# Perceiver block on one Trainium2 core: ten units of the V projection placed earlier in the instruction streams

## The reference, cut to what matters

```
x = x + depool(layernorm(x), ctx, lens)
x = x + mamba(layernorm(x))            # delta = softplus(...), scan over 64 tokens, 16 states
x = x + bitnet_ffn(layernorm(x))       # ternary weights, activations quantized per row
x = x + cross_attention(layernorm(x), ctx)   # K, V = ctx @ Wkv (16 heads of 64)
x = x + head_attention(layernorm(x))
x = x + experts(layernorm(x))
```

## Time and profile before

| | |
|---|---|
| median of 3 runs | 3235.72 us (3234.48 to 3242.55) |
| the profiled execution's own time | 3228.4 us |
| its span, first to last instruction | 3226.7 us |
| mean granted clock of TensorE | 0.957 of full |
| TensorE busy | 2927.9 us, 91% |
| VectorE busy | 1506.7 us, 47% |
| ScalarE busy | 1012.3 us, 31% |
| `mamba_in` softplus to its end | about 151 to 229 us |
| `mamba_scan` | 229 to 696.6 us |
| `mamba_out` and norm n2 | 696.6 to 753.6 us |
| `bitnet` | 753.6 to 910.6 us |
| `queries` with n3 | 910.6 to about 1415 us |

### The profile page before, as it was taken

The page is one execution under the profiler, slowest core; times in us unless marked ns, Lnnn a source line. Parts: engine busy times, 40 slices in busy tenths (PEclk is TensorE's granted clock), DMA queues, the critical chain, the costliest instruction groups (busy, mean ns, idle before and its releaser), DMA issues. The chain is left out here.

```text
span 3226.7 us, 40186 instructions
## 1 busy us (share of the span) xinstructions
PE 2927.9 (91%) x17021; PEld 1616.3 (50%) x17029; DVE 1506.7 (47%) x1769; ACT 1012.3 (31%) x1525; POOL 68.6 (2%) x189
## 2 busy tenths in 40 slices
PE   6979999977989999989999999999999997636799
PEld 3324444433444444446666666666666664415453
DVE  5359999974633222333434343434343432376410
ACT  3344334313422221222323232323232321284210
POOL 1000000000000000000000000000000000010000
PEclk9989999988999999999999999999999998867999
DMA  5123343333323333444556554546464543102203
GB/s 198 59 73 92 93 145 89 92 101 140 96 91 121 102 99 103 129 116 110 142 115 143 114 143 110 143 114 143 112 143 110 117 84 85 53 20 46 95 10 143
DMA packets 472619, 341.52 MB, mean 106 GB/s; under 512 B 232212, under 2 KB 437333, under 8 KB 467832
## 3 DMA queue, kind: packets, MB, share of 16 engines
q1 hardware_dynamic: 472440, 338.95, 38.7%
HBM read 226.60 MB, written 54.62 MB: 87 GB/s over the span
## 5 line engine op out<-in xcount | busy, mean ns | idle before, releaser
L366 PE MATMUL vw_pv<-vw_wv,vw_ctx 128*128 128x512 f16 (+1 forms) x1296 | 496.8, 383 | 63.0 <-DVE vw_vst L386 27.6
L367 PE MATMUL vw_pv<-vw_wv,vw_ctx 128*128 128x512 f16 (+1 forms) x1296 | 496.4, 383 | 0.0
L368 PE MATMUL vw_pv<-vw_wv,vw_ctx 128*128 128x512 f16 (+1 forms) x1296 | 495.5, 382 | 0.0
L1442 PE MATMUL ca_p_s<-early_halves,ca_qw 128*128 128x448 f16 (+2 forms) x1408 | 466.7, 331 | 1.4 <-DVE ca_qw L1555 1.4
L1443 PE MATMUL ca_p_s<-early_halves,ca_qw 128*128 128x448 f16 (+2 forms) x1408 | 466.7, 331 | 0.0
L1444 PE MATMUL ca_p_s<-early_halves,ca_qw 128*128 128x448 f16 (+2 forms) x1408 | 466.6, 331 | 0.0
L1555 DVE TENSOR_TENSOR ca_qw<-ca_p_w,ca_qw 128x512 f16<-128x512 f32 x128 | 88.5, 691 | 545.6 <-ACT ca_qw L1505 545.6
L386 DVE TENSOR_TENSOR vw_vst<-vw_pv,vw_vst 128x512 f16<-128x512 f32 x162 | 110.8, 688 | 376.9 <-ACT vw_vst L377 376.8
L1505 ACT ACTIVATE ca_qw<-ca_p_w 128x512 f16<-128x512 f32 x128 | 76.4, 597 | 558.8 <-PE ca_p_w L1423 558.8
L377 ACT ACTIVATE vw_vst<-vw_pv 128x512 f16<-128x512 f32 x162 | 95.4, 593 | 468.4 <-PE vw_pv L368 468.4
L366 PEld LDWEIGHTS vw_pv<-vw_wv,vw_ctx 128*128 128x128 f16 (+1 forms) x1296 | 127.7, 99 | 228.9 <-issue 39.9
(11 more groups left out here) (439 smaller groups left out, 4700.3 us busy)
## 6 DMA issues: line engine op xcount, KB each, us to landing
vw_ring<-in_ctx_t SPq DMA_DIRECT2D x109, 512.0 KB, 3.7
vd<-vw_vst SPq DMA_DIRECT2D x192, 256.0 KB, 2.3
ca_vals<-vd SPq DMA_DIRECT2D x64, 768.0 KB
ca_stage<-in_ctx_t SPq DMA_DIRECT2D x91, 512.0 KB, 3.6
ex_w_d<-in_w_d SPq DMA_DIRECT2D x8, 2048.0 KB, 7.1
early_r<-state_rows SPq DMA_DIRECT2D x8, 1024.0 KB, 8.1
early_r<-in_w SPq DMA_DIRECT2D x2, 4096.0 KB, 15.7
vw_ring<-in_w_kv SPq DMA_DIRECT2D x8, 512.0 KB, 4.7
```

Of the source, the lines that this page charges most:

```text
L366: self.nc.tensor.matmul(o, xh[:, c, 0:w], self.wv[0][:, c, f], start=(c == 0), stop=False)
L367: self.nc.tensor.matmul(o, xh[:, c, 0:w], self.wv[1][:, c, f], start=False, stop=False)
L368: last = self.nc.tensor.matmul(o, xl[:, c, 0:w], self.wv[0][:, c, f], start=False, stop=(c == CC - 1))
L1442: nc.tensor.matmul(o, a[:, 0, c, :], x[:, 0, c, lo:hi], start=(c == 0), stop=False)
```

## The change

Four edits. In `mamba_in` each softplus step takes three units in place of two on all four engines, and V has two more banks for the length of the stage, the unused banks 2 and 3 of `proj`. In `mamba_scan` four more units stand behind the last step on all four engines. In `bitnet` TensorE takes its first two units ahead of the wait for the quantized rows in place of behind the transposes; the other engines' order is as it was. The count of units before `queries` becomes 123. `queries` takes what is left: 79, of which 72 in a row behind the last projection.

```
@@ mamba_in
         p_dt = proj
-        STEP_UNITS = 2
+        STEP_UNITS = 3
+        banks = vw.banks
+        vw.banks = banks + [proj[:, i * BANK:(i + 1) * BANK] for i in (2, 3)]
...
             vw.dve(dve, STEP_UNITS)
 
+    vw.banks = banks
+
@@ mamba_scan
-    HALF, UNITS_PER_STEP = bc.HALF, 5
+    HALF, UNITS_PER_STEP, UNITS_BEHIND = bc.HALF, 5, 4
...
                         sp.dma_start(bc.c[q], bc.source(1, 1, q)).then_inc(bc.ld_c[q], 16)
+            vw.sp(sp, UNITS_BEHIND)
...
-            vw.pe(pe, STEPS * UNITS_PER_STEP)
+            vw.pe(pe, STEPS * UNITS_PER_STEP + UNITS_BEHIND)
...
                 vw.act(act, 3 - n % 2)
+            vw.act(act, UNITS_BEHIND)
...
                 nc.vector.tensor_tensor(delta[:, e, t], h[0][:, 0, :], h[0][:, 1, :], ALU.add).then_inc(summed, 1)
+            vw.dve(dve, UNITS_BEHIND)
@@ bitnet
+            vw.pe(pe, 2)
             pe.wait_ge(xq_ready, NT)
             for r in range(2):
...
                 last.then_inc(xt_ready, 1)
-            vw.pe(pe, 2)
             weight_sum(0)
@@ build
-                vw = ValueWork(nc, io, st, io.vd, wkt, halves, 115)
+                vw = ValueWork(nc, io, st, io.vd, wkt, halves, 123)
```

## The result

The changed kernel took 3190.33 us (median of 4 runs, 3187.50 to 3192.84), beside 3237.98 us for the kernel before (median of 4). The ratio is 0.9854, with a 95% interval of 0.9838 to 0.9869, or 42 to 52 us less. Forecast were 3191.8 us and a range of 3184 to 3204, so the time is inside the range, 1.5 us from the number. Two later comparisons of the same kernel on other occasions gave 0.9846 (0.9832 to 0.9860) and 0.9862 (0.9847 to 0.9876).

The account below looks back on a forecast made before the run. TensorE was taken to bound the tail, with pauses in softplus, at the scan's end and at `bitnet`'s head. -41.5 + 0.3 + 5.3 - 8.0 = -43.9 us, from 3235.7 to 3191.8 us; range 3184 to 3204 for eight in ten.

Parts of the forecast that it names:

- Tail: Behind the query projections, where TensorE is the bound: eight units fewer at 5.18 us each, 41.5 us less.
- Softplus: Softplus steps in `mamba_in`: four more units fill TensorE's waits for banks; the stage ends 0.3 us later.
- Behind the scan: End of `mamba_scan`: four more units, mostly hidden until VectorE's last sum; the next stage starts 5.3 us later.
- `bitnet`: Head of `bitnet`: two units moved ahead of the transposes; `first(0)` starts 8.0 us earlier.
- (a): Softplus and `bitnet`: about five short waits each cost a slow start of 2.1 us, +10.5, 3202 us; chance 0.06.
- (b): Softplus: added banks do not release TensorE, steps take 20.0 + 5.2, four units cost 20.7, 3212 us; chance 0.05.
- (c): `bitnet` gives nothing: the transposes' delay goes through to `first(0)`, rounding waiting for the weights; 3200 us; chance 0.06.
- (d): Units behind the scan find no cover; the stage grows some 22 us in place of 5.3, 3208 us; chance 0.03.
- (e): Slower: TensorE almost without rest is held at 1.2 GHz in the scan, up to 3627 us; chance 0.03.

Follow-up runs that it names:

- single edits: The kernel before with one edit each: softplus alone 3218.61 us, four units behind the scan alone 3225.06 us, `bitnet` transposes alone 3234.17 us.
- six-unit kernel: The changed kernel with six units behind the scan in place of four: 3192.61 us, ratio 0.9853 against the kernel before.
- four-unit kernel: The changed kernel with four units in a softplus step in place of three: 3212.05 us, ratio 0.9916 against the kernel before.
- five-unit variant: The changed kernel with five units behind the scan in place of four: 3185.66 us, ratio 0.9832, then 3183.03 us, 0.9824, against the kernel before.

## Why the prediction was right

- **Tail.** Forecast -41.5, in the trace -41.5 (414.7 to 373.2 us). With the query projections in front of it the difference is 41.1 us for the eight units, and 21.0 and 20.9 for four in the single edits: 5.1 to 5.3 us a unit.
- **Softplus.** Forecast +0.3 for the stage, +0.6 found, and its waits to within 0.2 us. The sum was right. What it did not say is how the gain divides: it priced the pauses as room for four units, while the banks alone are worth 12.7 us and the units only the rest. It named VectorE's chain of 15.2 us as something that has to keep up, but did not draw the conclusion that this is the step's length once the banks are there.
- **Behind the scan.** Forecast +5.3, found +5.4 (+5.1 alone). The 4.9 us of drain were 4.75, and the stage end on an item cost the 1.3 us that the earlier trace rows had shown elsewhere.
- **`bitnet`.** Forecast -8.0 to `first(0)`, found -8.2 (-8.0 with the missing record), but this exactness is partly luck, since the way there had errors that cancel. The two units took 12.8 us in place of 12.6. From the transposes to the next unit were 4.7 us in place of 5.5, since the transposes ran at the full clock (0.61 and 0.62 us in place of 1.03 each). The four units took 22.4 us where the forecast had 20.9 of work and 1.1 of waiting for a bank. That wait did not come up; in its place the clock fell behind the 2.16 us wait and cost 1.7 us, by which time the bank was free. In the six-unit kernel, where it did not fall, the bank wait is there (0.78 us) and the four units take 21.7: the fall costs 0.7 us net.
- **Not in the sum.** The output projection's stage gained 0.6, because its two units took 12.2 us in place of 12.8 behind the shorter pause, and 1.8 and 1.7 us were lost at slow clock behind `first(0)` and in norm n3. With 0.9 in the unedited rest this is 3.8 of the 4.2 us between the -43.9 forecast and the -39.7 of the two profiled executions. It is inside the range. The losses behind `first(0)` and in n3 are the clock's, see below; where the 0.9 comes from is open.
- **Rivals.** (a), that short waits cost clock: the waits of 0.31 and 1.43 us did not, nor did the 1.74 of the kernel before; the Trainium skill's rule ("TensorE: Matmul & The Clock Gate", "A second HAM failure mode: psum-queue depth-cycling") is not borne out at these lengths. For waits a little over 2 us the rival had a point. In the eight traces with the `bitnet` edit the clock fell behind the wait of 2.16 or 2.25 us for a bank in six. The forecast's evidence against it, three pauses without a fall, was also a choice: of six waits of 2.18 us in the scan of the kernel before, two were followed by a fall, with a first matmul of 0.57 us behind the one (at 499.81) and 0.39 behind the other:

```profile
556.92 0.39 PE L366 MATMUL ms_pv<-vw_wv,vw_ctx 128*128 128x512 f16 x1 [2.18 <-DVE vw_ctx L342]
```

```profile
556.92:567.90 10.98, 10.98 (x44) 4.64 (x45) 10.98 (x7) 5.18 (x11) 0.00 (x0) 0.84 0.49 140
```

- (b), (c) and (d) are out by the stage lengths. What (b) feared, a step whose first unit waits, does happen with one unit a step more: that is the four-unit kernel. (e): granted clock 0.960 to 0.965 over the span in the four runs, higher than the 0.957 before.
- On the medians the forecast hit to 1.5 us, which is partly luck. The kernel before measured 3238.0 in the final comparison and not 3235.7, so the change itself was 47.6 us on the medians and 39.7 in the traces, 3.7 more and 4.2 less than the 43.9 forecast. By the traces alone 3236 - 40 = 3196 would have been expected.

## What to carry to other kernels

Before filling an engine's pause with more work, look at what ends the pause. If it is a buffer, add the buffer and see how far the next chain lets the stage shrink; here that was two thirds of the gain, and the extra work only earned the rest. One buffer more than a step fills is what lets a step start at once: three units in four banks did not wait at the start of a step, four units in four banks waited 5.6 us, exactly as two in two. This is for units that are emptied one step after they are made. Background work behind a stage's last instruction is worth adding until its own end passes that of the stage, and it should end on the piece with the shortest drain.

## What the hardware did unexpectedly

Whether TensorE's clock falls around a pause of 2 to 3 us differs between kernels whose code is the same there, and between two executions of one kernel. Norm n3 in the first and the second trace of the five-unit variant, both behind a pause of 2.79 us, its two units at a granted clock of

```profile
904.84:915.19 10.35, 10.35 (x48) 4.74 (x49) 4.96 (x14) 1.30 (x2) 0.00 (x0) 1.00 0.55 204
```

and

```profile
904.71:916.75 12.04, 12.04 (x48) 5.13 (x49) 4.96 (x14) 1.30 (x2) 0.00 (x0) 0.86 0.47 176
```

The norm behind the output projection took 12.1 us for its two units in the kernel with softplus alone, behind 2.14 us, and 10.4 in the five-unit variant, behind 2.30: the longer pause is the one without a fall. The second product in `bitnet`, behind 2.52 us, took 5.1 to 5.3 us in nine traces and 3.6 in three. It is not a coin tossed each time either: the three traces of the changed kernel agree at all of these places (n3 12.2 us, the second product 5.3, the four units 22.4). What decides it is not shown.

Between the softplus steps and the cross attention, in all twelve traces, no wait of 0.3 to 1.92 us that began at the full clock was followed by a slow burst of units, and every burst behind a pause of 4.09 us or more was slow in part. And the forecast's test, the first matmul's duration, can mislead: in the kernel with the transposes' edit alone the first matmul behind a pause of 4.11 us took

```profile
753.15 0.38 PE L366 MATMUL vw_pv<-vw_wv,vw_ctx 128*128 128x512 f16 x1 [4.11 <-PEq L73]
```

and yet its two units took 12.2 us: the clock fell after the restart. One has to read the whole burst. A fall made two units take 11.8 to 13.0 us in place of 10.5, and a stage of many short dependent products, like head attention, differed by 4 to 5 us between two traces of one kernel. That is the scatter against which edits of a few microseconds have to be seen.
